# A conditioned transformer block on one core: first loads in another order, transposes of the identity at the start, and one product moved

## The chip, the cores and the metric

The kernel runs on one core of one Trainium2 chip. The metric is the device time of one execution in microseconds (us); lower is better. The kernel before takes 229.39 us, the median of 3 runs (228.8 to 229.43). Engines are named as in the profile: PE is TensorE's matmul, PEld its weight load, DVE VectorE, ACT ScalarE, POOL GpSimd, SP SyncE, which here only issues DMAs.

## What is computed

The reference, cut to the block itself, with x of 2 x 1024 x 256 and cond of 2 x 256, all in float32:

```
def rmsnorm(x, w):
    return x * jax.lax.rsqrt(jnp.mean(x * x, axis=-1, keepdims=True) + EPS) * w

def film(x, cond, w, b):
    ss = cond @ w + b
    scale, shift = jnp.split(ss, 2, axis=-1)
    return x * (1.0 + scale[:, None, :]) + shift[:, None, :]

h = film(rmsnorm(x, norm1_w), cond, film1_w, film1_b)
Q = h @ q_w + q_b
K = h @ k_w + k_b
V = h @ v_w + v_b
scores = jnp.einsum('bnd,bmd->bnm', Q, K) * D ** (-0.5)
attn = jax.nn.softmax(scores, axis=-1)
out = jnp.einsum('bnm,bmd->bnd', attn, V)
x = x_in + (out @ proj_w + proj_b)
x_in = x
h = film(rmsnorm(x, norm2_w), cond, film2_w, film2_b)
h = jax.nn.gelu(h @ mlp_w1 + mlp_b1, approximate=False) @ mlp_w2 + mlp_b2
return x_in + h
```

## The kernel before

The 2048 tokens are 16 tiles of 128 rows, in 4 groups of 4 tiles; groups 0 and 1 are the first sequence (b = 0), groups 2 and 3 the second. Weights are folded on the core: q_w times k_w (transposed) gives one matrix for G = h (Wq Wk^T), so that scores are G h^T, and v_w times proj_w gives one for V. Operands of large matmuls are split into a high and a low part, a product being three passes (L785). The high part is written by ScalarE or GpSimd, the low one by VectorE.

Every engine has a program written out by hand, and runs it in order; what orders the engines among each other are semaphores. The stretch that matters here is the start, up to the work on group 1:

- SyncE issues all loads on one queue, in the order of lines 201 to 215: the first half of group 0's x (2 tiles), its second half, the two halves of the q and k weights, the vectors (vcol, 11 KB), the conditioning rows (both, each broadcast to 128 partitions; L206), film1's transposed weights (512 KB; L207), the v and proj weights, x of group 1, k's weights and the bias rows, the output biases, x of groups 2 and 3, film2's weights. Then it waits for addrow_done (L217) and loads the first MLP weights.
- GpSimd makes the 128 x 128 identity (L270 to L273), then for each group the inverse root mean squares (inverse_rms, L283 and L286) and most of the normed rows xn (L299), and the high columns of h (L291). L307 makes bv_wide, the v bias spread over 128 columns.
- ScalarE squares the first two tiles of each group (L375), writes the high part of the folded q and k weights (L401, L402), and turns the transposed rows in PSUM into h_full, with the film coefficients as scale and bias (L383, columns); high_G (L389) and high_V (L396) follow for each group.
- VectorE (L579 on): squares of tiles 2 and 3 of group 0 (squares(0), L566), two normed rows (L550), film_products(0, 0) (four dot products of 256 with the conditioning row, L530), coefficients(0, 0) (L539, L542), the low part of the q and k weights (L588), squares(1), low_columns(0) (L573), three bias products (L596), the low part of the v weights (L599), one normed row of group 1 (L550), the output row (L605), L607, film_products(0, 1) and its coefficients, squares(2), low_G(0) (L613), and then group 1.
- TensorE: the folded q and k weights (L821), transposes of group 0's xn (transpose_rows(0), L777), the folded v weights (L830), the bias row's product (L835: bv_wide times the proj weights, into bank 7; its result, v's bias through proj, is added to the output bias by VectorE at L605), then for each group G (project_g, L797 and L803), the next group's transposes, and V (L785). Group 1's G waits until low_G(0) has read banks 2 and 3.

The two places around which the change turns, on VectorE and on TensorE:

```
squares(0)
normed_rows(0, 0, range(GT // 2))
dve.wait_ge(wide_in, 16)
dve.wait_ge(film_in[0], 16)
film_products(0, 0, g_place(LO))
coefficients(0, 0)
...
dve.wait_ge(addrow_done, 1)
dve.wait_ge(rows_in, 16)
dve.tensor_tensor(add_row[:, 0, :], bank(7, D), add_row[:, 0, :], ALU.add).then_inc(addrow_ready, 1)
```

## Time and profile before

| | us |
|---|---|
| median of 3 runs | 229.39 |
| the profiled execution | 229.35 |
| its span | 227.5 |
| TensorE busy in the span (matmul) | 215.7 (95%) |
| VectorE busy | 151.6 (67%) |
| ScalarE busy | 111.1 (49%) |
| GpSimd busy | 72.3 (32%) |

The span runs from the first to the last instruction of the profiled execution; times of rows count from its start. In a row of the timeline stand the start, the duration of the merged instructions, the engine, the line, the operation, what it writes and reads, how many, and in brackets how long the engine was idle before them and who ended that. TensorE executes an fp32 matmul as two records, so that four matmuls of L821 stand as x8; a transpose is one record.

### The profile page before, as it was taken

The page shows a single profiled execution, that of the slowest core. Times are in us where ns is not written, and L with a number is a line of the kernel's source. Part 1 is how long each engine was busy: PE and PEld are TensorE (multiplying, and loading weights), DVE is VectorE, ACT ScalarE, POOL GpSimd, SP SyncE. Part 2 cuts the span into 40 slices and gives each one's busy share as a digit, 9 for nine tenths or more (in the row PEclk, how much of TensorE's full clock was granted, in tenths as well). Part 3 has the DMA queues.
Part 4 walks back from the last instruction along what each step waited for, and adds up shares of the span by engine and source line. Part 5 has one row for each costly group of instructions (what it writes and reads, how often), then busy time and mean ns, then how long its engine had stood idle before and what let it go on. Part 6 is the DMA issues. An engine that isn't in the chain of part 4 may idle for free.

```text
span 227.5 us, 3463 instructions
## 1 busy us (share of the span) xinstructions
PE 215.7 (95%) x1260; PEld 188.1 (83%) x1260; DVE 151.6 (67%) x292; ACT 111.1 (49%) x207; POOL 72.3 (32%) x102
## 2 busy tenths in 40 slices
PE   0898999999999999999999999999999999999994
PEld 0677888897799999999999999888788878889993
DVE  0499875589799998899988973148624852445222
ACT  3157655334633355433368860494449444644440
POOL 1565763001366314752445316046004500200000
PEclk9999999999999999999999999999999999999999
DMA  5994001046866777763566462000610061002002
GB/s 166 339 411 194 3 0 46 0 156 198 274 207 215 250 231 251 232 201 119 173 221 209 133 192 79 3 0 0 225 54 0 6 218 53 3 0 92 0 3 92
DMA packets 18161, 29.86 MB, mean 131 GB/s; under 512 B 2144, under 2 KB 12128, under 8 KB 18016
## 3 DMA queue, kind: packets, MB, share of 16 engines
q1 hardware_dynamic: 15696, 21.25, 29.3%
q10 hardware_dynamic: 2448, 8.39, 9.8%
q8 instruction: 10, 0.16, 0.3%
q14 instruction: 7, 0.06, 0.1%
HBM read 17.58 MB, written 12.06 MB: 130 GB/s over the span
## 4 chain that ended last, share of the span: by engine, by line
PE 78%; DVE 12%; DMA 3%; ACT 2%; issue 2%; SPq 1%; ACTq 1%; DVEq 0%
PE psum L785 34%; PE psum L859 19%; PE psum L914 9%; PE psum L906 5%; PE psum L912 5%; DMA raw<-in_film_wT_dram 3%; PE psum L803 3%; ACT probs L425 2%; PE psum L797 2%; DVE row_max L652 2%; PE psum L777 1%; DVE x_rows L750 1%; SPq L195 1%; DVE raw L672 1%; DVE probsT L677 1%
## 5 line engine op out<-in xcount | busy, mean ns | idle before, releaser
L731 DVE TENSOR_TENSOR G_all<-probs,G_all 128x512 fp32r<-128x512 f32 x32 | 22.6, 717 | 44.4 <-ACT G_all L501 44.4
L859 PEld LDWEIGHTS psum<-V_all,probsT 128*128 128x128 f32 x384 | 47.4, 188 | 2.1 <-DVE probsT L677 0.8
L785 PE MATMUL psum<-hT,w 128*128 128x512 f32 x192 | 49.1, 392 | 0.0
L859 PE MATMUL psum<-V_all,probsT 128*128 128x256 f32 x384 | 48.0, 281 | 0.4 <-DVE probsT L677 0.4
L785 PE MATMUL psum<-hT,G_all 128*128 128x512 f32 x192 | 46.7, 393 | 0.0
L501 ACT ACTIVATE probs<-psum,vcol 128x512 f32<-128x512 f32 x32 | 22.0, 689 | 44.7 <-PE psum L785 44.3
L785 PEld LDWEIGHTS psum<-hT,G_all 128*128 128x128 f32 x192 | 35.0, 188 | 7.3 <-ACT probs L425 0.3
L785 PEld LDWEIGHTS psum<-hT,w 128*128 128x128 f32 x192 | 35.5, 188 | 6.8
L436 ACT CAST probsT<-keys_first 128x1024 fp32r<-128x1024 f32 x16 | 16.8, 1049 | 32.1 <-DVE raw L672 15.5
L341 POOL TENSOR_TENSOR x_rows<-x_rows,add_row 128x256 f32<-128x256 f32 x16 | 11.9, 742 | 63.8 <-DVE probsT L677 63.8
L914 PE MATMUL psum<-w,G_all 128*128 128x512 f32 x84 | 30.5, 398 | 0.0
L912 PE MATMUL psum<-w,G_all 128*128 128x256 f32 x96 | 26.7, 280 | 0.0
L291 POOL TENSOR_SCALAR hT<-h_full 128x512 fp32r<-128x512 f32 x16 | 11.3, 710 | 42.8 <-ACT h_full L470 33.8
L425 ACT ACTIVATE probs<-psum,exp_bias 128x1024 f32<-128x1024 f32 x16 | 17.9, 1121 | 9.6 <-DVE exp_bias L655 9.6
L501 ACT ACTIVATE G_all<-psum,vcol 128x512 fp32r<-128x512 f32 x32 | 21.8, 682 | 0.0
L652 DVE TENSOR_REDUCE row_max<-psum 128x1 f32<-128x1024 f32 x16 | 19.2, 1197 | 3.0 <-PE psum L785 3.0
L677 DVE TENSOR_TENSOR probsT<-keys_first,probsT 128x1024 fp32r<-128x1024 f32 x16 | 19.5, 1220 | 1.6 <-ACT probsT L436 0.9
L914 PEld LDWEIGHTS psum<-w,G_all 128*128 128x128 f32 x84 | 15.8, 188 | 3.7
L912 PEld LDWEIGHTS psum<-w,G_all 128*128 128x128 f32 x96 | 18.1, 189 | 0.9
L335 POOL TENSOR_TENSOR x_rows<-x_rows,add_row 128x256 f32<-128x256 f32 x16 | 13.8, 887 | 3.1 <-DVE xn L550 3.1
L573 DVE TENSOR_TENSOR hT<-h_full,hT 128x512 fp32r<-128x512 f32 x16 | 11.0, 714 | 3.0 <-POOL hT L291 3.0
L906 PEld LDWEIGHTS psum<-w,G_all 128*128 128x128 f32 x96 | 12.4, 191 | 0.5
(74 smaller groups left out, 256.7 us busy)
## 6 DMA issues: line engine op xcount, KB each, us to landing
keys_first<-crossing SPq DMA_DIRECT2D x64, 128.0 KB, 3.0
crossing<-raw ACTq DMA_DIRECT2D x8, 512.0 KB, 3.7
crossing<-turned ACTq DMA_DIRECT2D x7, 512.0 KB, 3.9
out_dram<-x_rows SPq DMA_DIRECT2D x7, 256.0 KB, 3.1
x_rows<-in_x_dram SPq DMA_DIRECT2D x3, 512.0 KB, 9.0
rows_crossing<-raw SPq DMA_DIRECT2D x3, 512.0 KB, 2.6
raw<-rows_crossing SPq DMA_DIRECT2D x12, 128.0 KB, 2.9
raw<-in_film_wT_dram SPq DMA_DIRECT2D x2, 512.0 KB, 8.6
```

What stands on the lines that cost most here:

```text
L335: pool.tensor_tensor(row, row, add_row[:, 1, :], ALU.add).then_inc(bias2_added, 1)
L425: act.activation(probs[:, parity, :], psum[:, 2 * parity:2 * parity + 2, :].rearrange("p a n -> p (a n)"), ACT.Exp, bias=exp_bias[:, t:t + ...
L436: act.copy(probsT[:, t % 2, HI, :, :].rearrange("p k (a n) -> p k a n", n=Q), keys_first[:, t % 2, :, :, :].rearrange("p a k n -> p k a n" ...
L501: act.activation(dst, bank(2 + m % 2), ACT.Gelu, bias=vcol[:, B1 + m:B1 + m + 1]).then_inc(gelu_done, 1)
L652: dve.reduce_max(row_max[:, col], psum[:, 2 * parity:2 * parity + 2, :].rearrange("p a n -> p (a n)"), AX_X, negate=True).then_inc(max_don ...
L677: dve.tensor_tensor(lo, keys_first[:, t % 2, :, :, :].rearrange("p a k n -> p k a n"), hi.bitcast(F32), ALU.subtract).then_inc(probsT_read ...
L731: dve.tensor_tensor(gelu[:, m, LO, :], gelu_full[:, m % 2, :], gelu[:, m, HI, :].bitcast(F32), ALU.subtract).then_inc(gelu_ready, 1)
L785: last = pe.matmul(dst, stationary(a, k), moving(b, k), start=(n == len(tiles) * len(PASSES) - 1), stop=(n == 0))
L859: last = pe.matmul(bank(6 + t % 2, D), probsT[:, t % 2, a, k, :], V_all[:, t // KT * KT + k, s, :], start=(n == 0), stop=(n == KT * len(PA ...
L906: last = pe.matmul(bank(4 + j, D), a, w2[:, m, b, :], start=(m == 0 and n == 0), stop=(m == HT - 1 and n == len(PASSES) - 1))
L912: last = pe.matmul(bank(4 + j, D), lo, w2[:, m, HI, :], start=False, stop=False)
L914: last = pe.matmul(bank(4 + j), hi, both, start=False, stop=(m == HT - 1))
```

## The change

The loads start with one conditioning row (128 KB as broadcast) and film1's weights (512 KB), with x behind them; the second conditioning row is a load of its own behind group 1's x. VectorE forms film_products(0, 0) ahead of x's squares and waits for the second row ahead of film_products(0, 1). TensorE waits for the identity first and transposes it 32 times into banks 0 and 1 before its first wait for weights. The two matmuls of the bias row's product stand behind G of group 0 and ahead of group 1's transposes. Lines of the changed kernel are 2 to 7 higher for the same statement (L566 is L569, L605 is L608, L821 is L828).

```
+    WARM = 32
...
+        cond_in = [sem(f"cond_in{b}") for b in range(B)]
...
+            load(cond_rows[0][:, 0:1, :], rows[0:1, :].partition_broadcast(P), cond_in[0])
+            load(film_wT[0], film1_wT, film_in[0])
             load(x_rows[:, 0:GT // 2, :], x_v[:, 0, 0:GT // 2, :], x_half_in)
             load(x_rows[:, GT // 2:GT, :], x_v[:, 0, GT // 2:GT, :], x_in[0])
             for e in range(DT):
                 load(qk_raw[:, e, :], qk_weights[:, e, :], wqk_in[e])
             load(vcol[:, :], vectors, vec_in)
-            load(cond_rows[0], rows[0:B, :].partition_broadcast(P), wide_in)
-            load(film_wT[0], film1_wT, film_in[0])
             load(raw[:, QK_END:VP_END], vp_weights, wvp_in)
             load_x(1)
+            load(cond_rows[0][:, 1:2, :], rows[1:2, :].partition_broadcast(P), cond_in[1])
             load(wk, k_w, k_in)
...
+            dve.wait_ge(cond_in[0], 16)
+            dve.wait_ge(film_in[0], 16)
+            film_products(0, 0, g_place(LO))
             squares(0)
             normed_rows(0, 0, range(GT // 2))
-            dve.wait_ge(wide_in, 16)
-            dve.wait_ge(film_in[0], 16)
-            film_products(0, 0, g_place(LO))
             coefficients(0, 0)
...
+            dve.wait_ge(cond_in[1], 16)
             film_products(0, 1, late_place)
...
-                        dve.wait_ge(wide_in, 32)
+                        dve.wait_ge(wide_in, 16)
...
+            pe.wait_ge(ident_ready, 1)
+            for n in range(WARM):
+                pe.transpose(bank(n % 2)[:, 0:P], ident[:, :], ident[:, :])
             for e in range(DT):
                 pe.wait_ge(wqk_in[e], 16)
...
-            pe.wait_ge(ident_ready, 1)
             transpose_rows(0)
...
-            pe.wait_ge(wide_ready, DT)
-            for e in range(DT):
-                last = pe.matmul(bank(7, D), bv_wide[:, e, :], wp[:, e, :], start=(e == 0), stop=(e == DT - 1))
-            last.then_inc(addrow_done, 1)
...
                 project_g(g)
+                if g == 0:
+                    pe.wait_ge(wide_ready, DT)
+                    for e in range(DT):
+                        last = pe.matmul(bank(7, D), bv_wide[:, e, :], wp[:, e, :], start=(e == 0), stop=(e == DT - 1))
+                    last.then_inc(addrow_done, 1)
                 if g + 1 < GROUPS:
                     pe.wait_ge(h_done, DT * (g + 1))
                     transpose_rows(g + 1)
```

TensorE, from its first matmul to the V matmuls of group 0, as it stands before (the names are those of the list above: raw holds the weights, probs bv_wide, probsT the folded weights, hT the columns of h):

```order
L821 MATMUL psum<-raw 128x258 [waits wqk_in0]
L821 MATMUL psum<-raw 128x258 [waits wqk_in1]
L777 MATMUL psum<-ident,xn 128x128 [waits xn_done,ident_ready]
L830 MATMUL psum<-raw 128x256 [waits wvp_in]
L835 MATMUL psum<-raw,probs 128x256 [waits wide_ready]
L797 MATMUL psum<-hT,probsT 128x512 [waits h_hi,qk_ready]
L803 MATMUL psum<-hT,probsT 128x512 [waits h_ready]
L777 MATMUL psum<-ident,xn 128x128 [waits xn_done,h_done]
L785 MATMUL psum<-probsT,hT 128x258 [waits addrow_ready,vp_ready]
```

The same stretch of TensorE with the change:

```order
L824 MATMUL psum<-ident 128x128 [waits ident_ready]
L824 MATMUL psum<-ident 128x128 x31
L828 MATMUL psum<-raw 128x258 [waits wqk_in0]
L828 MATMUL psum<-raw 128x258 [waits wqk_in1]
L781 MATMUL psum<-ident,xn 128x128 [waits xn_done]
L836 MATMUL psum<-raw 128x256 [waits wvp_in]
L801 MATMUL psum<-hT,probsT 128x512 [waits h_hi,qk_ready]
L807 MATMUL psum<-hT,probsT 128x512 [waits h_ready]
L872 MATMUL psum<-raw,probs 128x256 [waits wide_ready]
L781 MATMUL psum<-ident,xn 128x128 [waits xn_done,h_done]
L789 MATMUL psum<-probsT,hT 128x258 [waits addrow_ready,vp_ready]
```

The transposes of the identity (L824) are new and come first, and the bias row's product, L835, has become L872 between group 0's G (L807) and group 1's transposes; the V matmuls (L789) still wait for addrow_ready behind it.

VectorE from its start to the coefficients, before:

```order
L566 ISA V_all,sumsq<-x_rows 128x256 [waits x_in0]
L566 ISA V_all,sumsq<-x_rows 128x256
L550 TENSOR_SCALAR xn<-x_rows,rstd 128x256 [waits rstd_done]
L530 ISA G_all,film_sum<-raw,keys_first 128x256 [waits film1_in,wide_in]
L539 TENSOR_TENSOR coef<-film_sum,vcol 128x4 [waits vec_in,film_sums]
```

And with the change:

```order
L533 ISA G_all,film_sum<-raw,keys_first 128x256 [waits film1_in,cond_in0]
L569 ISA V_all,sumsq<-x_rows 128x256 [waits x_in0]
L569 ISA V_all,sumsq<-x_rows 128x256
L553 TENSOR_SCALAR xn<-x_rows,rstd 128x256 [waits rstd_done]
L542 TENSOR_TENSOR coef<-film_sum,vcol 128x4 [waits vec_in,film_sums]
```

The four film products (the first row of them stands here) are now ahead of x's squares; the order of VectorE behind the coefficients is the same as before.

## Rows read from the trace of the kernel before

**Rows 1.** The page's head, and the shares of the chain that ended last.
```profile
span 227.5 us, 3463 instructions
...
PE 78%; DVE 12%; DMA 3%; ACT 2%; issue 2%; SPq 1%; ACTq 1%; DVEq 0%
```

**Rows 2.** Chain of waits in order of time, 0 to 24 us: start, us, what.
```profile
3.52 6.65 DMA raw<-in_film_wT_dram
...
10.30 0.43 DVE G_all L530
...
16.70 0.52 issue
...
21.25 1.33 DVE G_all L613 x2
22.59 0.04 issue
22.63 1.19 PE psum L797 x4
```

**Rows 3.** Timeline, SyncE, GpSimd and VectorE, up to group 1's xn.
```profile
0.72 0.86 SPq L195 DMA_DIRECT2D x_rows<-in_x_dram  x2
...
1.16 0.29 POOL L273 TENSOR_SCALAR_AFFINE_SELECT ident<-ident 128x128 f32<-128x128 f32 x1 [0.20 <-POOL ident L270]
...
5.32 0.43 DVE L566 CUSTOM_DVE_ANT_0 V_all<-x_rows 128x256 fp32r<-128x256 f32 x1 [5.32 <-DMA x_rows<-in_x_dram]
...
7.72 1.11 POOL L299 TENSOR_SCALAR xn<-x_rows,rstd 128x256 f32<-128x256 f32 x2
...
16.73 1.43 POOL L299 TENSOR_SCALAR xn<-x_rows,rstd 128x256 f32<-128x256 f32 x3 [0.19 <-POOL rstd L286]
```

**Rows 4.** Timeline of TensorE's matmuls, 0 to 26 us.
```profile
6.34 3.81 PE L821 MATMUL psum<-raw 128*128 128x258 f32 x8 [6.34 <-DMA raw<-in_qk_weights_dram]
...
9.94 1.15 PE L777 MATMUL psum<-ident,xn 128*128 128x128 f32 x8
...
13.32 1.03 PE L835 MATMUL psum<-raw,probs 128*128 128x256 f32 x4
...
14.67 1.16 PE L797 MATMUL psum<-hT,probsT 128*128 128x512 f32 x4 [0.32 <-POOL hT L291]
...
15.72 2.13 PE L803 MATMUL psum<-hT,probsT 128*128 128x512 f32 x8
...
18.30 1.06 PE L777 MATMUL psum<-ident,xn 128*128 128x128 f32 x8 [0.46 <-POOL xn L299]
...
19.12 3.13 PE L785 MATMUL psum<-probsT,hT 128*128 128x258 f32 x24
...
23.83 2.13 PE L803 MATMUL psum<-hT,probsT 128*128 128x512 f32 x8
...
25.80 0.38 PE L777 MATMUL psum<-ident,xn 128*128 128x128 f32 x2
```

**Rows 5.** Timeline: the coefficients, h_full behind them, and the output row.
```profile
12.01 0.16 DVE L542 SCALAR_TENSOR_TENSOR coef<-coef,vcol 128x2 f32<-128x2 f32 x1
...
12.20 1.45 ACT L383 ACTIVATE h_full<-psum,coef 128x512 f32<-128x512 f32 x2 [1.57 <-DVE coef L542]
...
17.74 0.41 DVE L605 TENSOR_TENSOR add_row<-psum,add_row 128x256 f32<-128x256 f32 x1
```

**Rows 6.** Stretches: engines' busy us (instructions), granted clock, DMA share, GB/s.
```profile
0.00:2.00 2.00, 0.00 (x0) 0.00 (x0) 0.00 (x0) 1.27 (x1) 0.73 (x7) 1.00 0.06 18
2.00:4.00 2.00, 0.00 (x0) 0.00 (x0) 0.00 (x0) 0.01 (x1) 0.00 (x0) 1.00 0.80 199
4.00:6.00 2.00, 0.00 (x0) 0.00 (x0) 0.68 (x3) 0.91 (x4) 0.00 (x0) 1.00 0.99 298
6.00:7.00 1.00, 0.66 (x2) 0.57 (x3) 0.10 (x2) 0.00 (x0) 0.61 (x2) 1.00 0.97 173
7.00:8.00 1.00, 1.00 (x4) 0.81 (x3) 0.35 (x2) 0.00 (x0) 0.90 (x2) 1.00 0.90 236
8.00:9.00 1.00, 1.00 (x3) 0.81 (x3) 0.50 (x2) 0.00 (x0) 1.00 (x3) 1.00 1.08 438
```

**Rows 7.** Weight loads of L821 and L830: ns min/median/max, first and last start.
```profile
L821 PEld LDWEIGHTS psum<-raw x8: 289/337/338, 6.3 to 9.1; 128*128 128x128 f32 x8
...
L830 PEld LDWEIGHTS psum<-raw x8: 186/190/190, 11.5 to 12.9; 128*128 128x128 f32 x8
```

## The prediction

> **What bounds the kernel now.** I read the page's head first: the span is 227.5 us, and TensorE holds 78% of the chain that ended last [rows 1]. The profiled execution took 229.35 us, so 1.85 us lie around the span; the median of the runs shown is 229.39 us, 0.04 us above it. I make the sum against 229.35 and add the 0.04 at the end. The rest of the chain lies mostly at its start, and nothing behind group 0 is touched by the change, so what counts is when the work of group 1 begins. I therefore read the chain of waits from the start to 24 us [rows 2]: the load of film1's weights until 10.17, the four film products on VectorE, then, piece after piece, VectorE alone from 10.30 to 22.6 us, up to the second low_G (L613). Only then does TensorE begin group 1 (L797 at 22.63) and stay the bound. The reader should see there the first and the last of those pieces; of the some 50 between, none is another engine's and the longest that is no work is 0.52 us. Whatever lets VectorE arrive at L613 earlier or later moves the end by as much.
>
> What feeds VectorE: the second load of x lands at 5.3 and starts the squares, and GpSimd ends its two rows of xn at 7.72 + 1.11 = 8.83 [rows 3]. TensorE could transpose them then, but is still in L821 and starts at 9.94 [rows 4]. The transposes are through by 11.09, the coefficients (L542) only at 12.17, and so ScalarE's first h_full starts at 12.20 [rows 4, 5]. Call that start T. From T on: TensorE's L797 at T + 2.47, L803 behind it until 17.85 [rows 4]. The bias row's product (L835, 13.32 to 14.35) is hidden in TensorE's wait for T's columns, and L605, which reads it, starts at 17.74 without having waited for it [rows 4, 5].
>
> **The loads in another order.** What is dropped: nothing. What moves: 640 KB (one conditioning row broadcast to 128 partitions, 128 KB, and film1's 512 KB) goes ahead of x. film_products(0, 0) then runs on VectorE before x's squares, while VectorE waits anyway. That takes 1.4 us (L530, four times 0.35, from 10.30) out of the row of VectorE work that starts T [rows 2]. But T now waits for x. The path from x's landing is: squares to GpSimd's last xn, 8.83 - 5.32 = 3.51; to the start of the transposes 0.15 (xn of group 1 ends at 18.16, its transposes start at 18.30), the transposes 1.06 (that same group's), ScalarE's start behind them 0.1 [rows 3, 4]. So T = X + 4.83, X being the landing of x's second half; the old T of 12.20 is met at X = 7.4.
>
> When is X? Ahead of it and with it 1.18 MB must move instead of 0.52 MB. In the trace of before the same two x loads needed from about 1.7 us (the stretch up to 2.0 has moved only 36 KB) to 4.3, by adding up the stretches, and landed at 5.3: 1.0 us behind the bytes [rows 3, 6]. Bounds: by the full rate of the stretch from 8 to 9 us, 438 GB/s, the 1.14 MB missing at 2.0 are moved by 4.6 and land at 5.6; I take 5.8 as the early end since each load is only issued some 0.47 us after the one before. By the curve of before itself 1.18 MB are reached at 6.9, landing at 7.9, the late end [rows 6]. That curve holds a dip (173 and 236 GB/s from 6 to 8 us) in the stretch of the small vector load and the broadcast of both rows, and the small load now stands behind x. I take film1's 0.52 MB at the full rate (1.2 us; its rows are 4 KB a partition like those moving from 8 us on) and the other 0.66 MB at the 205 GB/s at which x moved at the start (3.2 us): 1.7 + 4.4 + 1.0 = 7.1, and round it down to **X = 7.0**, for part of the start-up cost is paid once. T = 11.85, that is 0.35 earlier. film1's weights should land some 1.5 us ahead of X, just enough for the 1.4 us of products. The coefficients need vcol, which is now behind 0.51 MB of weights after x: about 9, while VectorE gets there at X + 3.4; not late. x of group 1 has 128 KB less ahead of it and comes no later than now. The second conditioning row is used only behind L605 (17.74), and from k's weights on the queue has as many bytes ahead of it as before: hidden.
>
> **The 32 transposes of the identity.** They start when the identity stands, at 1.5 us [rows 3], and write banks 0 and 1, which nothing needs then. Of TensorE's two levels, 2.4 GHz is what the rows from L830 on show: there the 128-wide weight load takes 190 ns at the median, and four records of L835 take 1.03 us; in L821, the first work, the load takes 337 ns and eight records 3.81 us, 0.48 each, about twice as long, so they ran at 1.2 GHz, although the granted clock reads 1.00 in every stretch [rows 4, 6, 7]. The first transposes of xn behind it, 8 in 1.15 us, are already near the 1.06 us of the later ones. One transpose takes 0.11 us at the full level (from 18.30 to the next work at 19.12, 0.82 for 8) and, as an estimate, twice that at the slow one. The 32 are therefore over between 5.0 us (32 x 0.11) and 8.5 us (32 x 0.22); if they raise the clock on their way, well before the first qk weights arrive (about 8). L821's four matmuls then need 2 us in place of 3.8, end at about 10 and are out of the way of the transposes at X + 3.7 = 10.7. So they cost nothing and gain nothing beyond what T = X + 4.83 takes for granted; the first rival is what happens otherwise.
>
> **The bias row's product behind G of group 0.** This is the term that counts. L605 stands in VectorE's queue between L550 and L607; queued behind it are the second four film products, the coefficients, squares(2) and low_G(0), for which TensorE's group 1 waits; ScalarE's high_G(0) waits for L607. The product now starts when the last matmul of L803 is issued. L797 to L803 is 1.05 us apart, L803 to what follows it 1.9 (in group 1 it is 1.97, from 23.83 to the transposes at 25.80), the product itself 1.03 [rows 4]: its end is T + 2.47 + 1.05 + 1.9 + 1.03 = T + 6.45. With the old T that is 18.65, against 17.74, when L605 starts today: **+0.9 us**. VectorE is idle meanwhile (without the wait it would be there by 17.74 at the latest) and has no other work in order. The transposes of group 1 slip from 18.30 to about 18.5 and are needed only by ScalarE after high_G(0): covered. The load of w1, which waits for the same product, is issued 4 us later, and GpSimd reads it only once the first crossed probabilities are ready, behind all four groups: covered.
>
> **Sum.** +0.9 for the wait at L605, -0.35 for the earlier T: +0.55, or in one line S = X - 6.45. Nothing behind L613 gives it back: TensorE's holes at 22.63 and the work after it are waits for the same VectorE. 229.35 + 0.55 + 0.04 = 229.94, so **230.0 us**.
>
> **Rival 1, slower: the transposes don't raise the clock.** Then the 32 go at the slow level to the end, 32 x 0.22 = 7.0 us, until 8.5, by which time the first qk weights are there. L821 runs as now, 3.8 us at the slow level, and the transposes of xn start 3.6 us behind its start [rows 4], at 11.9 to 12.2, last 1.15 as today, and T is 13.2 to 13.45. S = +0.9 + 1.15 = **+2.1: 231.5 us**, up to 2.7 if the slow level lasts into the transposes. It decides from the point where L821 ends later than X + 3.7. For it: no row shows transposes alone raising anything; the rise came with matmuls ahead. Against it: at the full level transposes keep TensorE as densely at work as matmuls do, eight in 1.06 us [rows 4]. The Trainium skill, in "TensorE: Matmul & The Clock Gate", part 4 on transposes, says that "HAM K=8/8 doesn't engage for transpose-mode", which speaks against this change; by that rule the time would be this rival's, while the transposes in this trace, amid matmuls, ran at the pace of the full clock.
>
> **Rival 2, better: x comes early.** If the start-up is a fixed delay and film1 and x move at the full rate, X = 5.8 and S = -0.65: **228.7 us**. It decides from X below 6.45, where the product's wait is paid for. For it: 438 GB/s later; against it: 199 and 298 GB/s from 2 to 6 us [rows 6]. The Trainium skill's page "DMA: Bandwidth & Descriptors", on the anatomy of one DMA, gives about 2.0 us plus bytes at 436 GB/s; by it x would land at 0.72 + 2.0 + 2.7 = 5.4, an estimate from that page, while for before's 0.52 MB it gives 3.9 and the trace has 5.3.
>
> **Rival 3, slower: x comes later still.** The broadcast of a row into 128 partitions is itself the dip from 6 to 8 us, and now stands first. X = 8.2, S = +1.75: **231.1 us**.
>
> **Chances.** Forecast 0.48 (X between 6.3 and 7.8: 229.3 to 230.8), rival 1 0.30, rival 2 0.14, rival 3 0.08. A measurement of this kernel can tell some 0.3%, 0.7 us, from no change. Slower by over that: rivals 1 and 3 and the part of the forecast with X over 7.15, 0.20, in all 0.58. Faster by over that: the better half of rival 2 and what I overlook there, 0.10. Within: 0.32. The range leaves out a tenth on either side: 229.0 to 231.9.
>
> **What would show it.** In the profile of the changed kernel: the squares of x's second half start at 7.0 (5.8 to 7.9); film products end before them; L821's records about 0.25 us apart and the weight load 188 ns, not 337; h_full at 11.9; VectorE idle 1 us or more ahead of the add_row instruction, released by TensorE's bias product at 18.3; L613 and the start of group 1 0.55 later than 22.63. The prediction is wrong if VectorE doesn't wait there, if x's squares start outside 5.8 to 7.9, or if the time after 24 us isn't simply shifted.

## The result, and the profile after

The changed kernel takes 230.56 us at the median of 20 runs, the kernel before, timed beside it, 229.38: 1.0052 times as long, 95% interval [1.0042, 1.0063]. That is 1.18 us slower. The forecast was 230.0, so the sign and the range held and the size was half of what came. The profiled execution took 230.48 us, with a span of 228.7 against 227.5.

Head of the changed kernel's profile, and each engine's busy time:

```profile
span 228.7 us, 3528 instructions
...
PE 219.7 (96%) x1292; PEld 193.2 (84%) x1292; DVE 150.5 (66%) x292; ACT 110.9 (48%) x207; POOL 72.5 (32%) x102
```

TensorE is 4 us busier because the transposes of the identity count as work (6.55 us, while the first matmuls behind them take 1.8 us less); that says nothing of the end. The chain of waits of the changed kernel, from the start to group 1 (start, us, what), answers to [rows 2]:

```profile
2.09 5.51 DMA x_rows<-in_x_dram
...
7.63 0.43 DVE V_all L569
...
12.39 0.79 ACT h_full L386
...
13.25 0.62 POOL hT L294
...
13.92 1.16 POOL hT L294
...
15.22 1.17 PE psum L801 x4
...
18.26 0.88 PE psum L872 x4
...
19.16 0.04 DVE add_row L608
...
22.65 1.33 DVE G_all L616 x2
...
24.02 1.19 PE psum L801 x4
```

Read it from the top. The chain now starts with x and not with film1's weights. It passes through the bias row's product (L872), which was hidden before, and through add_row on VectorE. Group 1 starts at 24.02, against 22.63. The timeline of the same kernel (start, us, engine, line, and in brackets idle time and who ended it) has the waits, and group 2's transposes, which will matter below:

```profile
5.93 0.42 DVE L533 CUSTOM_DVE_ANT_0 G_all<-raw,keys_first 128x256 fp32r<-128x256 f32 x1 [5.93 <-DMA raw<-in_film_wT_dram]
...
7.63 0.43 DVE L569 CUSTOM_DVE_ANT_0 V_all<-x_rows 128x256 fp32r<-128x256 f32 x1 [0.22 <-DMA x_rows<-in_x_dram]
...
18.10 1.03 PE L872 MATMUL psum<-raw,probs 128*128 128x256 f32 x4
...
19.16 0.42 DVE L608 TENSOR_TENSOR add_row<-psum,add_row 128x256 f32<-128x256 f32 x1 [1.34 <-PE psum L872]
...
27.18 1.04 PE L781 MATMUL psum<-ident,xn 128*128 128x128 f32 x8
```

L605 started at 17.74 without a wait [rows 5]; L608 starts at 19.16, 1.42 later, and VectorE is idle for 1.34 us ahead of it. The 1.42 splits into three:

- ScalarE's h_full starts at 12.39 in place of 12.20: 0.19.
- TensorE's L801 starts 2.83 behind h_full in place of 2.47: 0.36. GpSimd's second high column takes 1.16 us, its first 0.62.
- The rest, 0.87, is the product: L801 to L608 is 3.94 us, and L797 to L605 was 3.07.

From there the delay is carried on: group 1 is 1.39 late, group 2's transposes 1.38 (27.18 against 25.80 [rows 4]). The span grew by 1.2 only. The missing 0.2 has a place. Behind the first row_max of the attention, ScalarE issues two DMAs. The second of them took 0.99 us in the profile of before and 0.33 in that of after:

```profile
46.61 0.99 ACTq L445 DMA_DIRECT2D crossing<-turned  x1
```

```profile
47.98 0.33 ACTq L448 DMA_DIRECT2D crossing<-turned  x1
```

That is 0.66 us less on ScalarE, of which about 0.15 reaches the work behind it: ScalarE's next exponential starts at 49.40 in place of 48.17, 1.23 late, where the issue itself was still 1.37 late. The experiments with the transposes (e4 and e12 below) show that this belongs to the change.

### The profile page after: what moved, and what is told of

Read it like the earlier page. It is cut to its first block, busy times and chain, and to the rows that moved or that the text cites. A ratio compares the mean times of both kernels' runs of the same rounds, so it can differ in the third digit from the quotient of the medians.

```text
span 228.7 us, 3528 instructions
## 1 busy us (share of the span) xinstructions
PE 219.7 (96%) x1292; PEld 193.2 (84%) x1292; DVE 150.5 (66%) x292; ACT 110.9 (48%) x207; POOL 72.5 (32%) x102
## 4 chain that ended last, share of the span: by engine, by line
PE 79%; DVE 10%; ACT 2%; DMA 2%; issue 2%; POOL 2%; SPq 1%; ACTq 0%; POOLq 0%
PE psum L789 34%; PE psum L861 19%; PE psum L921 9%; PE psum L913 5%; PE psum L919 5%; PE psum L807 3%; DMA x_rows<-in_x_dram 2%; PE psum L801 2%; DVE row_max L656 2%; ACT probs L428 2%; PE psum L781 2%; DVE x_rows L754 1%; DVE raw L676 1%; DVE probsT L681 1%; PE psum L918 1%
## 5 line engine op out<-in xcount | busy, mean ns | idle before, releaser
L789 PE MATMUL psum<-hT,w 128*128 128x512 f32 x192 | 49.1, 393 | 0.0
L789 PE MATMUL psum<-hT,G_all 128*128 128x512 f32 x192 | 46.5, 393 | 0.0
L789 PEld LDWEIGHTS psum<-hT,w 128*128 128x128 f32 x192 | 35.5, 188 | 6.7
L789 PEld LDWEIGHTS psum<-hT,G_all 128*128 128x128 f32 x192 | 35.0, 188 | 7.1 <-ACT probs L428 0.2
```

The source lines that it names most:

```text
L789: last = pe.matmul(dst, stationary(a, k), moving(b, k), start=(n == len(tiles) * len(PASSES) - 1), stop=(n == 0))
```

## The experiments

All were timed against the kernel before on the same chip, each in 5 to 12 executions. Ratio is to that kernel; the times behind it are those of one profiled execution: when x's squares start on VectorE, when h_full starts (called T), when the output row is formed, when group 1's G starts, when group 2's transposes start, and the span.

| | median us | ratio [95%] | x | T | row | G of group 1 | transposes of group 2 | span |
|---|---|---|---|---|---|---|---|---|
| before | 229.38 | | 5.32 | 12.20 | 17.74 | 22.63 | 25.80 | 227.5 |
| after | 230.56 | 1.0052 [1.0042, 1.0063] | 7.63 | 12.39 | 19.16 | 24.02 | 27.18 | 228.7 |
| e1 product back | 229.81 | 1.0018 [1.0005, 1.0032] | 7.66 | 12.42 | 17.77 | 22.58 | 26.41 | 228.0 |
| e2 product only | 230.33 | 1.0045 [1.0029, 1.0061] | 5.34 | 12.16 | 18.70 | 23.56 | 26.74 | 228.8 |
| e3 no transposes | 232.24 | 1.0117 [1.0097, 1.0137] | 7.56 | 13.18 | 19.95 | 24.82 | 27.98 | 229.8 |
| e4 transposes only | 229.06 | 0.9980 [0.9964, 0.9996] | 5.51 | 12.23 | 17.76 | 22.64 | 25.81 | 227.3 |
| e5 loads only | 231.90 | 1.0103 [1.0072, 1.0135] | 7.64 | 13.18 | 18.53 | 23.33 | 27.15 | 229.3 |
| e6 x, then film | 229.24 | 1.0009 [0.9983, 1.0035] | 5.38 | 12.41 | 17.81 | 22.70 | 25.87 | 227.4 |
| e7 products early | 230.49 | 1.0048 [1.0033, 1.0064] | 7.85 | 12.61 | 18.35 | 22.94 | 27.24 | 228.8 |
| e8 both | 232.22 | 1.0117 [1.0088, 1.0146] | 5.41 | 12.39 | 19.56 | 24.07 | 28.38 | 229.9 |
| e9 low columns later | 229.42 | 1.0003 [0.9986, 1.0021] | 8.17 | 12.93 | 18.47 | 23.36 | 26.52 | 228.1 |
| e10 film behind qk | 228.85 | 0.9973 [0.9956, 0.9991] | 5.43 | 11.86 | 17.39 | 21.83 | 25.80 | 227.5 |
| e11 row first | 228.67 | 0.9964 [0.9943, 0.9984] | 6.87 | 12.15 | 17.68 | 22.57 | 25.73 | 227.3 |
| e12 eight transposes | 228.96 | 0.9981 [0.9968, 0.9994] | 5.41 | 11.93 | 17.46 | 22.35 | 25.52 | 227.1 |

The column to watch is the one ahead of the span. In every row the span ends 201.5 to 202.2 us behind the start of group 2's transposes, whatever group 1's G did: e1 and before start that G within 0.05 us of each other and end 0.5 apart. The four rows without any transposes of the identity (before, e2, e3, e5) have 201.7 to 202.2 there, the ten with them 201.5 to 201.7. A profile is one execution: with the same order of loads x stands at 7.56 to 8.17 in six of them (after, e1, e3, e5, e7, e9), so that differences of a few tenths in x and T alone say little; intervals from T on are safer.

### Is it the product? e1 and e2

e1 is the changed kernel with the product at its old place, e2 the kernel before with the product moved. The main theory was that the wait for the product is nearly all of the loss; the rival that the late x is. e1's edit against the changed kernel (e2's, against before, is its reverse):

```
+            pe.wait_ge(wide_ready, DT)
+            for e in range(DT):
+                last = pe.matmul(bank(7, D), bv_wide[:, e, :], wp[:, e, :], start=(e == 0), stop=(e == DT - 1))
+            last.then_inc(addrow_done, 1)
...
                 project_g(g)
-                if g == 0:
-                    pe.wait_ge(wide_ready, DT)
...
-                    last.then_inc(addrow_done, 1)
```

> The changed kernel with the bias row's product back at its old place, behind the folded v weights. Theory W (the time is lost where VectorE waits for the product): TensorE has room for it, from the end of the v weights at 14.0 to G at 15.2 us, so the add_row instruction follows its predecessor at about 17.9 us instead of 19.16, group 1's G starts at about 22.7 instead of 24.02, and the time is 229.5 us, within 0.2 of before. Rival L (the later landing of x is what costs): 230.3 us or more, as the changed kernel.

> The kernel before with only the bias row's product moved behind G of group 0. Theory W: h_full still starts at 12.2, the add_row instruction at 18.65 instead of 17.74, group 1's G at 23.5 instead of 22.63, 230.2 us (+0.8 to +0.9). Rival L: 229.4 us, no change.

The timeline of e2: the product behind G of group 0, VectorE waiting for it, group 1 late.

```profile
17.64 1.03 PE L866 MATMUL psum<-raw,probs 128*128 128x256 f32 x4
...
18.70 0.42 DVE L605 TENSOR_TENSOR add_row<-psum,add_row 128x256 f32<-128x256 f32 x1 [0.93 <-PE psum L866]
...
23.56 1.20 PE L797 MATMUL psum<-hT,probsT 128*128 128x512 f32 x4 [1.15 <-DVE G_all L613]
```

The product's move costs 1.0 us by itself, and the place is the predicted one: add_row at 18.70, where the prediction had 18.65. In e1 that wait is gone, and still 0.48 of the 1.18 us stay, though group 1's G starts at 22.58, no later than before. That lies between the two theories, 229.5 and 230.3. The timeline of e1 shows what is late instead:

```profile
13.28 1.82 POOL L294 TENSOR_SCALAR hT<-h_full 128x512 fp32r<-128x512 f32 x2 [1.39 <-ACT h_full L386]
...
15.25 1.18 PE L801 MATMUL psum<-hT,probsT 128*128 128x512 f32 x4 [0.34 <-POOL hT L294]
...
22.50 1.33 POOL L289 TENSOR_TENSOR rstd<-meansq,power 128x4 f32<-128x4 f32 x1
...
24.01 2.26 POOL L302 TENSOR_SCALAR xn<-x_rows,rstd 128x256 f32<-128x256 f32 x4 [0.18 <-POOL rstd L289]
...
26.41 1.06 PE L781 MATMUL psum<-ident,xn 128*128 128x128 f32 x8 [0.65 <-POOL xn L302]
```

Group 2's transposes wait for GpSimd's xn; before they came straight behind G, at 25.80. So there are two paths side by side from T to group 2: VectorE's row of work up to low_G, and GpSimd's row of high columns, rstd and xn. The product lengthens the first, and the second too, since ScalarE's high_G of group 0 waits for L607, right behind add_row. The loads lengthen the second: T is 0.2 late, the two high columns take 1.82 us in place of 1.46, and the rstd for group 2 takes 1.33 in place of 1.01. In e1 VectorE's low columns of group 1 start ahead of that rstd (22.29), in before behind it (22.50); it takes 1.34 in e5 and 1.36 in e10, and 1.01 in the changed kernel. GpSimd's rows of before, the rstd and the xn of group 2:

```profile
22.09 1.01 POOL L286 TENSOR_TENSOR rstd<-meansq,power 128x4 f32<-128x4 f32 x1
...
23.28 2.23 POOL L299 TENSOR_SCALAR xn<-x_rows,rstd 128x256 f32<-128x256 f32 x4 [0.18 <-POOL rstd L286]
```

Group 2's transposes are 0.94 late in e2 and 0.61 in e1, and 1.38, not 1.55, in the changed kernel, for the later of the two paths counts. It is more than the larger of the two, since the moved product waits for a G of group 0 that the loads have made 0.55 late (15.22 for 14.67). The medians, 1.0 and 0.48 against 1.18, can't be added up as they stand: e1 and the changed kernel hold a gain of the transposes that e2 doesn't have (e12 below).

### What do the transposes do? e3, e4 and e5

e3 is the changed kernel without the 32 transposes, e4 the kernel before with them, e5 the changed kernel without them and with the product back, so that only the loads are left. The transposes write nothing that the result needs. The edit of e3 and e5 against the changed kernel (e5 has e1's too); e4 adds the same lines to before:

```
-            for n in range(WARM):
-                pe.transpose(bank(n % 2)[:, 0:P], ident[:, :], ident[:, :])
```

> The changed kernel without the 32 transposes of the identity. If they raised TensorE's clock: the q and k weights' eight records take 3.8 us instead of 2.0 (8.5 to 12.3), the transposes of xn start at 12.1 instead of 11.20, h_full at 13.4 instead of 12.39, and the time is 1.0 us more, 231.5 us. If the clock would have risen anyhow or is off the path: 230.5 us.

> The kernel before with only the 32 transposes at TensorE's start. They last until 8.1 us, while the first weights are there at 6.3; the q and k weights then take 2.0 us at the higher clock and end at 10.1, against 10.15 before. h_full waits for the coefficients until 12.2 all the same: 229.4 us, no change. A gain of 0.5 us or more would mean that TensorE's clock at the start bounds the kernel before; a loss that the transposes are in the way.

> The changed kernel without the transposes of the identity and with the product back at its old place: only the order of the loads, and with it of the film products, is left of the change. The q and k weights run at the slow clock from 8.5 to 12.3 us, h_full starts at 13.4. The product, behind the v weights, ends at about 16.0 and is no longer waited for; low_columns and all behind them on VectorE come 1.0 us later than in the changed kernel with the product back, so group 1's G starts at 23.6 to 23.8: 230.4 us. If the slow clock is hidden there: 229.5 us.

Whether transposes of the identity raise TensorE's clock can be read from them directly. By line, ns min/median/max, the changed kernel's transposes from 2 to 7.2 us and those from 7.3 on:

```profile
L824 PE MATMUL psum<-ident x26: 402/421/422, 1.8 to 7.1; 128*128 128x128 f32 x26
```

```profile
L824 PE MATMUL psum<-ident x7: 272/273/421, 6.9 to 7.8; 128*128 128x128 f32 x7
```

One takes 421 ns until about 7.1 us and 273 after: TensorE had done nothing but transposes since 1.51, and went from its 1.2 to its 2.4 GHz level on them. The granted clock reads 1.00 throughout. The moment differs from one execution to the next: in the nine profiles with 32 transposes the first fast one starts between 5.0 and 7.3 us, the transposes being TensorE's only work until then in all of them. The first work on weights finds the fast level there. Weight loads of the first matmuls, with the transposes and without them (e3):

```profile
L828 PEld LDWEIGHTS psum<-raw x8: 186/190/190, 8.5 to 9.9; 128*128 128x128 f32 x8
```

```profile
L826 PEld LDWEIGHTS psum<-raw x8: 289/335/338, 8.6 to 11.3; 128*128 128x128 f32 x8
```

Timeline of e3: the first matmuls take 3.62 us in place of 2.01, and h_full starts at 13.18 in place of 12.39.

```profile
8.58 3.62 PE L826 MATMUL psum<-raw 128*128 128x258 f32 x8 [8.58 <-DMA raw<-in_qk_weights_dram]
...
13.18 1.45 ACT L386 ACTIVATE h_full<-psum,coef 128x512 f32<-128x512 f32 x2 [0.49 <-PE psum L781]
```

In the changed kernel the transposes are worth 1.7 us (232.24 to 230.56), where 1.0 was expected. About half of it, 0.8, stands at T. With the product at its old place they are worth 2.1 us: e5 was expected at 230.4 and took 231.90, against 229.81 for e1, although G of group 1 starts at 23.33, ahead of the 23.6 expected. In e5's profile, as in e1's, group 2's transposes (27.15) wait for GpSimd. The profiled executions of e3 and e5 are their fastest (231.60 of 231.60 to 232.37, and 231.13 of 231.13 to 232.94), so where all of the rest goes in the usual execution isn't seen. In the kernel before (e4) they move no row of the start, all within 0.03 us from T on: there T waits for film1's weights. I had expected nothing, and yet e4 is 0.2% faster.

### Why are the transposes worth something where the start doesn't move? e12

ScalarE's second DMA issue is long (0.97 to 1.29 us) in exactly the four profiles without transposes, and 0.33 in all others. In the profile of before, a 16 KB packet of a queue of instructions starts between 46.2 and 46.4 us, just ahead of that issue at 46.61. Its share there, 29.6% of 16 engines for 0.2 us, is 0.95 us of one of them, so it is still moving while ScalarE issues. In the other three profiles without transposes it starts 0.19 to 0.35 us ahead of the issue as well, in the ten with them 3.2 to 8.3 us ahead, and is over by then. In e4 it starts between 38 and 39. Only TensorE's program was lengthened, so it is that program being loaded, piece by piece. If that is the cause, a few transposes do as well as 32, whatever TensorE's clock does. e12 is e4 with 8 of them.

```
+            pe.wait_ge(ident_ready, 1)
+            for n in range(8):
+                pe.transpose(bank(n % 2)[:, 0:P], ident[:, :], ident[:, :])
```

> The kernel before with 8 transposes of the identity in place of 32, ahead of the first wait for weights. What it is for: in the profiles of the kernels without the 32 transposes, ScalarE's second DMA issue of the attention (46.61 in before) takes 0.97 to 1.29 us, in those with them 0.33; in before a 16 KB packet of a queue of instructions moves between 46.2 and 46.4, in the one with 32 transposes it moves between 38 and 40. Theory F (fetch): the transposes shift the place of TensorE's program at which the next piece of it is loaded, and with it the packet, away from that issue. 8 transposes shift it by a quarter, some 1.8 us, to about 44.5: the issue takes 0.33, and the time is that of the 32, 229.0 to 229.1 for 229.35. Theory C (clock): the gain is from what TensorE's clock does at the start. 8 transposes end near 4.9 us without having raised the clock, the first matmuls still take 3.8 us, the issue takes 0.99 and the time is that of before. Under both, h_full at 12.2 and group 1 at 22.6.

DMA queues of before from 46.2 to 46.4 us, and of e12 from 43 to 44 (packets, MB, share of 16 engines); then the issue in e12 and its first matmuls' weight loads:

```profile
q8 instruction: 1, 0.02, 29.6%
```

```profile
q8 instruction: 1, 0.02, 7.8%
```

```profile
46.32 0.33 ACTq L445 DMA_DIRECT2D crossing<-turned  x1
```

```profile
L824 PEld LDWEIGHTS psum<-raw x8: 246/335/339, 6.1 to 8.8; 128*128 128x128 f32 x8
```

The median weight load is still 335 ns, so the clock at the start is as slow as in before; the packet has moved to 43 to 44, between e4's place and before's; the issue takes 0.33; and the gain is e4's, 0.9981 for 0.9980. Where the gain arises can be read on ScalarE, in the first exponential behind the issue, in before and in e4:

```profile
48.17 1.14 ACT L425 ACTIVATE probs<-psum,exp_bias 128x1024 f32<-128x1024 f32 x1
```

```profile
48.03 1.12 ACT L425 ACTIVATE probs<-psum,exp_bias 128x1024 f32<-128x1024 f32 x1 [0.41 <-DVE exp_bias L655]
```

Both issues start at 46.61; behind them e4 is 0.14 ahead, and its span ends up 0.18 shorter. In e2, whose issue takes 1.29, 0.3 more than before's, the delay grows there from 0.93 to 1.26 us. So the place where a piece of TensorE's program is loaded decides, not the clock. What in that load makes ScalarE's issue long isn't seen. The rows ahead of it are 0.28 us earlier than before's in e12's profile, since film1's weights landed earlier in it: that is no effect of 8 transposes, the other expectations on the start (12.2, 22.6) being met by e4. The changed kernel has this gain too, so its loads and its product cost more than the 1.18 us that are left.

### Can the second film products be formed earlier? e6, e7 and e8

If VectorE's row were what counts, its second four film products (L533, 1.4 us) could be taken out of it. VectorE is idle for 1.27 us ahead of its first low column; e7 puts them there. e6 keeps the old product and puts x ahead of the conditioning row and film1's weights. e8 is both. e6 against e1:

```
-            load(cond_rows[0][:, 0:1, :], rows[0:1, :].partition_broadcast(P), cond_in[0])
-            load(film_wT[0], film1_wT, film_in[0])
             load(x_rows[:, 0:GT // 2, :], x_v[:, 0, 0:GT // 2, :], x_half_in)
             load(x_rows[:, GT // 2:GT, :], x_v[:, 0, GT // 2:GT, :], x_in[0])
+            load(cond_rows[0][:, 0:1, :], rows[0:1, :].partition_broadcast(P), cond_in[0])
+            load(film_wT[0], film1_wT, film_in[0])
...
-            film_products(0, 0, g_place(LO))
             squares(0)
             normed_rows(0, 0, range(GT // 2))
+            film_products(0, 0, g_place(LO))
```

e7 against e1:

```
             squares(1)
+            dve.wait_ge(cond_in[1], 16)
+            film_products(0, 1, late_place)
+            coefficients(0, 1)
             low_columns(0, slice(0, GW))
```

> The changed kernel with x loaded first, then the conditioning row and film1's weights, then the q and k weights; film products behind the normed rows again; product at its old place; the 32 transposes kept. x's second half lands at 5.3 us, film1's weights at about 7.6, the q and k weights at 8.5. The film products and coefficients are done by about 10.4, TensorE's q and k weights at 10.5, the transposes of xn at 11.5, h_full starts at 11.6 instead of 12.2 (before). Theory W with T as the start: 0.5 to 0.7 us faster than before, 228.8 us. Rival (VectorE's later work or group 1's x bounds whatever T is): 229.4 us.

> The changed kernel with the product at its old place and the second four film products with their coefficients moved from behind the add_row instruction to behind squares(1), where VectorE is idle in the changed kernel (12.6 to 13.9 and 14.6 to 15.1 us). VectorE then has 1.7 us less between add_row and low_G(0). If VectorE alone paces group 1: its G starts 1.4 us earlier than with the product back alone, at 21.3, 228.1 us. If TensorE's transposes and V of group 0 take over as the bound (18.7 to 22.9 us): G of group 1 at 22.6 or later and 229.3 us.

> Both of the former: x first with film1 behind it, product at its old place, second film products early. h_full starts at 11.6; TensorE's G of group 0 ends at 17.5, transposes and V of group 0 at 21.9, and group 1's G follows them at once: 228.6 us. If VectorE still is late at low_G(0): as x first alone, 228.8 us or more.

e7 was expected to gain or break even, and lost 1.3 us (0.7 against e1). The row of VectorE is shorter, as meant: low_G ends at 21.0 and G of group 1 starts at 22.94, straight behind V of group 0 on TensorE, as its second case had it. But the end is later than that case's 229.3. The chain of e7 shows who decides:

```profile
20.97 0.62 POOL hT L294
...
21.63 1.16 POOL hT L294
...
22.87 0.71 POOL meansq L286
...
24.85 1.05 POOL xn L302 x2
...
27.24 1.06 PE psum L781 x8
```

Every link up to TensorE is GpSimd's, and its second column of group 1 takes 1.16 in place of 0.62. VectorE, now with nothing else in its row, started its low column level with it, at 21.62 for 21.63. e8 was expected at 228.6 and took 232.22; its group 2 starts at 28.38, the latest of all. There x of group 1 lands so late (12.78) that VectorE has no idle stretch to fill. Two of its film products ran beside GpSimd and took 0.82 us in place of 0.42, its first low column came only behind them, at 16.06, and TensorE waited for it in the middle of group 0's G:

```profile
17.40 2.13 PE L807 MATMUL psum<-hT,probsT 128*128 128x512 f32 x8 [1.31 <-DVE hT L576]
```

Behind that, e8 meets e7's second high column as well (the two of group 1 take 1.83 us). So VectorE's row was not the only bound, and emptying it makes the other one longer.

e6 gave 229.24, no difference, where 228.8 was expected. x is there at 5.38, but the q and k weights are now behind the 640 KB (timeline of e6), and T is no earlier than in e1:

```profile
9.43 2.01 PE L828 MATMUL psum<-raw 128*128 128x258 f32 x8 [1.70 <-DMA raw<-in_qk_weights_dram]
```

### Is it the collision with GpSimd? e9

e9 is e1 with one wait more: VectorE starts its low columns only once both high columns are written. It makes VectorE later.

```
             squares(1)
+            dve.wait_ge(h_hi, DT)
             low_columns(0, slice(0, GW))
```

> The changed kernel with the product back at its old place (229.81 us), and VectorE waits for both high columns of group 0 instead of one before its first low_columns. Theory G (a second path runs through GpSimd: beside VectorE's low_columns its second high column took 1.16 us instead of some 0.65, and the normed rows of groups 1 and 2 follow on GpSimd): the two high columns take 1.3 to 1.4 us instead of 1.82, G of group 0 starts at 14.8 instead of 15.25, the transposes of group 1 at 18.4 instead of 18.80, those of group 2 at 26.0 instead of 26.41, and the time is 229.4 us. If VectorE's own path is what is left (rival V), waiting longer can only cost: 229.8 us or more.

Timeline of e9, to be held against that of e1 above:

```profile
13.79 1.29 POOL L294 TENSOR_SCALAR hT<-h_full 128x512 fp32r<-128x512 f32 x2 [1.40 <-ACT h_full L386]
...
15.11 1.29 DVE L576 TENSOR_TENSOR hT<-h_full,hT 128x512 fp32r<-128x512 f32 x2 [1.94 <-POOL hT L294]
...
15.22 1.16 PE L802 MATMUL psum<-hT,probsT 128*128 128x512 f32 x4
```

The two high columns take 1.29 us in place of 1.82, and TensorE's G starts 2.29 behind T in place of 2.83. From T to group 2's transposes it is 13.6 us (e1: 14.0; before: 13.6), and the median is 0.4 below e1's, level with before. Only intervals are read here, since the profiled execution is the slowest of e9's twelve (229.88) and x came late in it, at 8.17: its G and its transposes stand 0.4 to 0.6 us behind the expected times. The two were timed against medians of before of 229.40 and 229.33; the intervals of their ratios overlap, but ten of e9's twelve executions are faster than every one of e1's. A second witness is e6: T is 12.41, as in e1, but x of group 1 keeps VectorE at its squares until 13.5; the two high columns take 1.33 us, and group 2's transposes start at 25.87 in place of 26.41. The collision is the 0.36 of the result's sum. The Trainium skill, "SBUF — State Buffer", section "Who interferes with whom", says that a VectorE instruction with two inputs in SBUF contends with a GpSimd instruction that reads SBUF, and that the order of issue decides who blocks. This case's traces agree: the low column (h_full minus its high part) has two such inputs, in the changed kernel it starts at 13.91, GpSimd's second column at 13.92, and 0.62 becomes 1.16. In before GpSimd's high columns were there first, and it was VectorE's second square that met them and took 0.82 in place of 0.41:

```profile
13.07 1.46 POOL L291 TENSOR_SCALAR hT<-h_full 128x512 fp32r<-128x512 f32 x2 [3.50 <-ACT h_full L383]
```

```profile
13.22 0.82 DVE L566 CUSTOM_DVE_ANT_0 V_all<-x_rows 128x256 fp32r<-128x256 f32 x1
```

### A better start: e10 and e11

e10 loads x, the q and k weights, and then row and film1's weights. e11 loads the conditioning row, x, film1's weights, the q and k weights. Both have the transposes, the product at its old place, and film products behind x's squares.

```
e10: x, x, qk, qk, cond row 0, film1, vectors, ...
e11: cond row 0, x, x, film1, qk, qk, vectors, ...
```

> Loads in the order x, q and k weights, one conditioning row, film1's weights, vectors, v and proj weights, group 1's x, second conditioning row; the product at its old place and the 32 transposes kept; film products behind the normed rows. film1's weights land at 9.3 to 9.6 instead of 10.17 us, the coefficients are done at 11.3, h_full starts at 11.4 to 11.7 instead of 12.2, and group 1's x lands 0.3 earlier. If VectorE's row of work is the bound from there: 0.4 to 0.6 us faster than before, 228.8 us. If group 1's x (landing at 12.5) or GpSimd's rows bound it: 229.1 us.

> The changed kernel with only the conditioning row ahead of x, and film1's weights behind x, ahead of the q and k weights; the product at its old place; film products behind the normed rows. It measures what the row alone does to x's landing. By bytes alone (0.13 MB more, at 205 GB/s) x's second half lands at 6.0 us instead of 5.4; if the broadcast of a row is slow in itself (as from 6 to 8 us in the kernel before) at 6.9 or later. With x first it was 5.4, with row and film1 first 7.6. The q and k weights land at about 9.4 as with x first, so the time is that of x first, 229.2 us, in either case.

e10 took 228.85 us, the 228.8 that was expected if VectorE's row is the bound. Its profiled execution, the slowest of twelve (229.26), shows GpSimd as the bound all the same. Timeline of e10: G of group 1 starts 0.8 us earlier than in before, and group 2's transposes exactly when they did, with a wait for GpSimd.

```profile
21.83 1.20 PE L801 MATMUL psum<-hT,probsT 128*128 128x512 f32 x4
...
25.80 1.06 PE L781 MATMUL psum<-ident,xn 128*128 128x128 f32 x8 [0.65 <-POOL xn L302]
```

That is the plainest sight of the second path. The rstd ahead of that xn takes 1.36 us, again behind VectorE's low columns. e10's median is 0.55 below before's 229.40, and 0.2 of it is what e4 and e12 have; what its faster executions did at this place isn't seen. e11 settles what holds x up. Its timeline:

```profile
6.87 0.43 DVE L569 CUSTOM_DVE_ANT_0 V_all<-x_rows 128x256 fp32r<-128x256 f32 x1 [6.87 <-DMA x_rows<-in_x_dram]
```

x lands at 5.38 with nothing ahead (e6), at 6.87 with only the broadcast row ahead, 128 KB, and at 7.63 with film1's 512 KB too. The row costs 1.5 us, four times its size in film weights only 0.8. Each is read from one profile per order; x ahead of all else stood at 5.32 to 5.51 in seven, behind both at 7.56 to 8.17 in six, so the 1.5 is clear and the 0.8 rough. e11 has the lowest median here, 228.67 us, 0.9964 [0.9943, 0.9984] of before, below the 229.2 expected in either case. Of the 0.36%, 0.2 is what e4 and e12 have too. The rest has little to show for it: group 2's transposes start 0.07 us earlier than before's, and the profiled execution (229.08) is one of the slower of its runs. The intervals of e4, e10 and e11 overlap.

## Why the prediction was right, and where it was off

**The product behind G: right in place, price and cover.** +0.9 was predicted. e2 has add_row at 18.70 for 18.65, a wait of 0.93, +1.0 us. In the changed kernel the term measures 0.87. VectorE's idle ahead of add_row was to be 1 us or more, and is 1.34.

**x's landing: mis-sized.** X was set at 7.0 and is 7.63, inside the bounds 5.8 to 7.9. The step that failed is "the other 0.66 MB at the 205 GB/s at which x moved at the start (3.2 us)": it prices the broadcast row by its bytes, 0.6 us, and e11 shows 1.5; film1's weights, entered with 1.2, cost 0.8. The stretch from 2 to 4 us moved 161 GB/s where before moved 199 [rows 6]; film1's weights then ran faster than that (columns: engines' busy us, granted clock, DMA share, GB/s):

```profile
2.00:4.00 2.00, 2.00 (x11) 2.00 (x11) 0.00 (x0) 0.01 (x1) 0.00 (x0) 1.00 0.65 161
4.00:6.00 2.00, 2.00 (x11) 2.00 (x10) 0.07 (x1) 0.00 (x0) 0.00 (x0) 1.00 0.94 344
```

Rival 3 had the mechanism (the broadcast is itself slow) but put X at 8.2. Rival 2, X = 5.8, is out. The Trainium skill's formula named there ("DMA: Bandwidth & Descriptors", "Anatomy of one DMA — SWDGE (gpsimd) path") gives an estimate of 5.4 for x in this order; here it is 7.6. By its heading it is for DMAs that GpSimd issues, and SyncE issues these. The film products end before the squares start (0.22 us idle between them), as foretold.

**T = X + 4.83: right.** 7.63 + 4.83 = 12.46, measured 12.39. So the loads bring T 0.19 later, where -0.35 was entered: with X mis-sized, this term has the wrong sign.

**T + 2.47 for L797: mis-sized, 2.83.** The interval was carried over from [rows 4, 5] as if it were a constant. It was short because VectorE was still at squares when GpSimd wrote its high columns. Moving film_products(0, 0) ahead emptied VectorE's row there, so it came early and blocked GpSimd's second column. Each instruction of the step was counted; who is beside whom was not.

**S = X - 6.45.** With the measured X it gives 1.18, the measured difference. That is in part luck: the 0.36 of the collision was missing in it, T came 0.07 earlier than the sum has it, and 0.2 was given back behind 24 us by the short DMA issue. "Nothing behind L613 gives it back" is therefore wrong too: the 32 transposes were costed only by what they do at the start, and not by what 32 more instructions do to the place of all later ones.

**"Whatever lets VectorE arrive at L613 earlier or later moves the end by as much": wrong.** It holds for later (e2: 0.93 at G, 0.94 at group 2's transposes). For earlier it fails: e10's profile arrives 0.8 earlier and gains nothing there, e7 has a shorter row and loses. In e1 the same time of arrival ends 0.5 later. The chain names one path; GpSimd's lay close behind it, in the profile of before 23.28 + 2.23 = 25.51 for an xn that TensorE took up at 25.80. Of these 0.29 us the start of the transposes takes 0.14 (26.27 to 26.41 in e1), so only some 0.15 us stood between them.

**The transposes: forecast right, rival 1 wrong.** L828's weight load takes 190 ns (188 foretold, 337 for the rival), eight records 2.01 us. The Trainium skill, "TensorE: Matmul & The Clock Gate", part 4, has it that the full clock doesn't engage for transposes; 32 of them alone, in fp32, engaged it here, and the measurement decides. "They cost nothing and gain nothing" held at the start and missed the 0.2% that e4 and e12 found. The 32 took 6.55 us, between the 3.5 and 7.0 that the estimates of 0.11 and 0.22 us for one give; they overlap, and one starts every 0.213 us at the slow level and every 0.115 at the fast one.

**The remaining covers held.** The q and k weights at 8.5 (about 8), group 1's transposes at 18.96, and vcol, the second row and w1 were never waited for in the rows above.

**The signs.** The squares at 7.63 and VectorE's wait of 1.34 us are within what was named. h_full came at 12.39 for 11.9, add_row at 19.16 for about 18.3, and group 1 started 1.39 later where 0.55 was named.

## What to carry over

A chain of waits names the latest path, not how close the next one is. Before a delay or a gain is carried to the end, follow the other engines' rows to the same meeting point and write down the slack; of two lengthened paths that don't touch each other the larger counts, not the sum. And taking work out of an engine's row moves all that follows into other neighbours: an interval copied from the trace holds only as long as the same instructions run beside it. Where two kernels differ in their number of instructions, look for differences at places that the change doesn't touch before you call them noise.

## What the hardware did that I had not expected

- A broadcast of one row of 1 KB to 128 partitions, as the first load, holds the next load up by 1.5 us (x at 6.87 for 5.38); 512 KB of weights add some 0.8.
- Transposes alone brought TensorE from 421 to 273 ns a transpose, while the granted clock read 1.00 before and after.
- A wait added to VectorE made the kernel 0.4 us faster (e9 against e1), since it keeps two instructions of 0.7 and 0.6 us from running side by side: GpSimd's took 1.16 beside VectorE's, and VectorE's film products 0.82 in place of 0.42 beside GpSimd.
- Eight more instructions at the start of TensorE's program change the length of a DMA issue on ScalarE 45 us later, 0.33 us for 0.99. In the four profiles in which a piece of that program is being loaded at that moment the issue is long, in the ten others it is short. It is worth 0.2% here.
